# The first ten jobs of a fused RWKV kernel: token mixing moved from VectorE into the weights of keys and receptance

## The reference

```python
for l in range(L):
    h = layernorm(x, ln1_w[l], ln1_b[l])
    hh = time_shift(h)                       # the token before
    xk = h * tmk[l] + hh * (1 - tmk[l])
    xv = h * tmv[l] + hh * (1 - tmv[l])
    xr = h * tmr[l] + hh * (1 - tmr[l])
    k = jnp.einsum('btc,oc->bto', xk, Wk[l])
    v = jnp.einsum('btc,oc->bto', xv, Wv[l])
    sr = jax.nn.sigmoid(jnp.einsum('btc,oc->bto', xr, Wr[l]))
    rwkv = sr * wkv(time_decay[l], time_first[l], k, v)
    x = x + jnp.einsum('bto,co->btc', rwkv, Wo[l])
    ...
```

## Time and profile before

| | |
|---|---|
| median of three runs | 1414.1 us (1412.24 to 1419.84) |
| the profiled execution | 1414.5 us, its span 1413.1 us |
| PE busy | 1305.1 us (92%) |
| DVE busy | 1280.8 us (91%) |
| ACT busy | 1253.0 us (89%) |
| POOL busy | 1179.1 us (83%) |
| granted clock of PE, mean | 0.982 of full speed |
| chain of work that ended last | PE 63%, DVE 24%, ACT 3%, POOL 2% |

### The profile page before, as it was taken

One profiled execution on the slowest core, in us unless ns is written; L12 is line 12 of the kernel. 1 busy time (PEld: TensorE's weight loads), 2 busy tenths in 40 slices (PEclk: granted clock), 3 DMA queues, 4 the chain that ended last, 5 costly groups with the idle time before them and its releaser, 6 DMA issues.

```text
span 1413.1 us, 23624 instructions
## 1 busy us (share of the span) xinstructions
PE 1305.1 (92%) x7245; PEld 931.7 (66%) x7245; DVE 1280.8 (91%) x2185; ACT 1253.0 (89%) x2525; POOL 1179.1 (83%) x1227
## 2 busy tenths in 40 slices
PE   2568899999999999999999999989999999889996
PEld 1235567767666766666666776767677888666775
DVE  6999999999999999999999999569999666699995
ACT  6789999999999999999999998977777888967864
POOL 6999999999999999999998999879988534478874
PEclk9879999999999999999999999999999999999999
DMA  7000000001000000000000000010000000001001
GB/s 230 0 1 1 1 2 1 1 2 32 1 2 1 1 1 1 1 1 1 1 1 1 1 1 16 24 31 22 17 1 1 1 1 1 1 8 31 23 29 33
DMA packets 26924, 18.55 MB, mean 13 GB/s; under 512 B 1072, under 2 KB 26160, under 8 KB 26800
## 3 DMA queue, kind: packets, MB, share of 16 engines
q1 hardware_dynamic: 26800, 17.05, 4.1%
HBM read 12.85 MB, written 4.19 MB: 12 GB/s over the span
## 4 chain that ended last, share of the span: by engine, by line
PE 63%; DVE 24%; issue 7%; ACT 3%; POOL 2%; DMA 0%; DVEq 0%; SPq 0%; ACTq 0%; POOLq 0%
PE ps L1129 14%; PE ps L1112 13%; PE ps L1029 4%; PE ps L1119 4%; PE ps L1099 3%; PE ps L1082 3%; PE ps L1068 3%; PE ps L1075 3%; PE ps L1076 3%; DVE hsc L248 3%; PE ps L1238 2%; PE ps L1167 2%; PE ps L1220 2%; DVE W L455 2%; DVE W L485 2%
## 5 line engine op out<-in xcount | busy, mean ns | idle before, releaser
L1112 PE MATMUL ps<-xk,W 128*128 128x512 f32 x512 | 266.3, 603 | 1.4 <-DVE W L455 1.4
L1129 PEld LDWEIGHTS ps<-W,kf 128*128 128x128 f32 x2048 | 244.9, 192 | 31.2 <-issue 30.1
L1129 PE MATMUL ps<-W,kf 128*128 128x128 f32 x2048 | 250.4, 276 | 0.0
L748 ACT ACTIVATE z<-X,ln_rs 128x128 f32<-128x128 f32 x512 | 233.0, 667 | 4.3 <-POOL ln_rs L597 4.3
L855 ACT ACTIVATE kf<-ps 128x512 f32<-128x512 f32 x256 | 195.9, 765 | 3.1 <-PE ps L1112 3.1
L1029 PE MATMUL ps<-idn,z 128*128 128x128 f32 x664 | 106.1, 285 | 61.4 <-DVE aa L358 39.5
L1029 PEld LDWEIGHTS ps<-idn,z 128*128 128x128 f32 x664 | 83.3, 147 | 119.2 <-issue 61.2
L862 ACT ACTIVATE kf<-kf 128x1024 f32<-128x1024 f32 x128 | 158.1, 1235 | 0.0
L1112 PEld LDWEIGHTS ps<-xk,W 128*128 128x128 f32 x512 | 88.0, 194 | 58.6 <-issue 56.6
L704 POOL TENSOR_TENSOR W<-W,hsc 128x704 f32<-128x704 f32 x64 | 88.7, 1386 | 45.1 <-DVE W L485 45.1
L595 POOL TENSOR_TENSOR ln_rs<-ln_rs,mhalf 128x8 f32<-128x8 f32 (+1 forms) x70 | 124.5, 1779 | 0.0
(11 more groups left out here) (168 smaller groups left out, 3986.9 us busy)
## 6 DMA issues: line engine op xcount, KB each, us to landing
X<-x_in SPq DMA_DIRECT2D x16, 256.0 KB, 6.9
xi<-x_in SPq DMA_DIRECT2D x16, 256.0 KB, 2.9
out<-X SPq DMA_DIRECT2D x16, 256.0 KB, 2.3
W<-weights SPq DMA_DIRECT2D x4, 832.0 KB, 8.4
W<-fp4w SPq DMA_DIRECT2D x1, 560.0 KB, 3.7
row<-rows SPq DMA_DIRECT2D x1, 192.0 KB, 3.0
wqkv<-qkv SPq DMA_DIRECT2D x1, 96.0 KB, 5.9
idn<-ident SPq DMA_DIRECT2D x1, 64.0 KB, 2.8
```

Source lines behind the costliest of these rows:

```text
L748: last = e.activation(chunk(dst, j), chunk(src, j), ACT.Identity, bias=rs[:, 1, j:j + 1], scale=rs[:, 0, j:j + 1])
L1112: e.matmul((pF0, pF1)[f % 2][:, :], w_of(r, WCK + f), xk[r % 2][:, :], start=True, stop=True).then_inc(kf_mm[f], 1)
L1129: last = e.matmul(chunk(pKV, j), kf[r % 3][:, f, j * 128:(j + 1) * 128], w_of(r, WCV + f), start=f == 0 and j == 0, stop=f == 3, skip_grou ...
```

## The change

For jobs 0 to 9 (all of layer 0) keys and receptance are computed as the values are: each as two products on the unmixed h1, one with the weights times tm on h1[:, 1:], the other with the weights times (1 - tm) on h1[:, :-1]. These four matrices WE lie in `big` and are written by four multiplications of 128x128 in `prepare_layer` for layer 0; omt now holds 1 - tm for all three factors. In jobs 0 to 9 `mix_t`, `mix_rt` and `sub_dh1` do nothing. h1 gets a third buffer, and the waits of `keep_h1` reach back one job further. `tanh_r` gets a wait, since the tile sr is no longer written by `mix_rt` before. A wait in `keep_hq` goes; GAP has the value of NB.

```diff
+EARLY = 10
+GAP = NB
...
-        h1, h2 = ring("h1", 2, [128, T + 1]), ring("h2", 2, [128, T + 1])
+        h1, h2 = ring("h1", 3, [128, T + 1]), ring("h2", 2, [128, T + 1])
...
+        WE = big[:, 0, :].rearrange("p (k c) -> p k c", k=4)
...
-        PADS = 3 + 10
+        PADS = 3 + 11
...
-                e.tensor_scalar(omt[:, :], vec[:, TMV, :], -1.0, 1.0, ALU.mult, ALU.add).then_inc(omt_done, 1)
+                e.tensor_scalar(omt[:, :, :], vec[:, TMK:TMR + 1, :], -1.0, 1.0, ALU.mult, ALU.add).then_inc(omt_done, 1)
...
+                if l == 0:
+                    for k, (matrix, mix) in enumerate(((WK, TMK), (WR, TMR))):
+                        e.tensor_scalar(WE[:, 2 * k, :], wk(matrix), vec[:, mix, 0:1], None, ALU.mult)
+                        e.tensor_scalar(WE[:, 2 * k + 1, :], wk(matrix), omt[:, mix - TMK, 0:1], None, ALU.mult).then_inc(we_done, 1)
...
             def mix_t(r):
-                if 0 <= r < NR:
+                if EARLY <= r < NR:
...
             def mix_rt(r):
-                if 0 <= r < NR:
+                if EARLY <= r < NR:
...
             def sub_dh1(r):
-                if 0 <= r < NR:
+                if EARLY <= r < NR:
...
             def keep_h1(r):
                 if 0 <= r < NR:
                     w.wait_ge(consts, PADS)
-                    w.wait_ge(v_mm, r - 1)
-                    w.wait_ge(xt_done, r - 1)
-                    w.wait_ge(xr_done, r - 1)
+                    w.wait_ge(v_mm, r - 2)
+                    w.wait_ge(k_done, min(r - 2, EARLY))
+                    w.wait_ge(r_mm, min(r - 2, EARLY))
+                    w.wait_ge(xt_done, r - 2 - EARLY)
+                    w.wait_ge(xr_done, r - 2 - EARLY)
                     w.wait_ge(turned1, r + 1)
...
             def tanh_r(r):
                 if 0 <= r < NR:
+                    w.wait_ge(p_done, r - 2)
                     w.wait_ge(r_mm, r + 1)
...
-                    w.wait_ge(p_turned, NT * NB if n >= NB else 0)
...
             def keys(r):
...
-                    w.wait_ge(xt_done, r + 1)
-                    e.matmul(pK[:, :], w_of(r, WK), xt[r % 2][:, :], start=True, stop=True).then_inc(k_done, 1)
+                    if r < EARLY:
+                        w.wait_ge(we_done, 1)
+                        w.wait_ge(h1_done, r + 1)
+                        e.matmul(pK[:, :], WE[:, 0, :], h1[r % 3][:, 1:T + 1], start=True, stop=False)
+                        e.matmul(pK[:, :], WE[:, 1, :], h1[r % 3][:, 0:T], start=False, stop=True).then_inc(k_done, 1)
+                    else:
+                        w.wait_ge(xt_done, r + 1 - EARLY)
+                        e.matmul(pK[:, :], w_of(r, WK), xt[r % 2][:, :], start=True, stop=True).then_inc(k_done, 1)
...
             def receptance(r):
                 if 0 <= r < NR:
                     w.wait_ge(*bR.hand_over(sr_done, r + 1))
-                    w.wait_ge(xr_done, r + 1)
-                    e.matmul(pR[:, :], w_of(r, WR), sr[r % 3][:, :], start=True, stop=True).then_inc(r_mm, 1)
+                    if r < EARLY:
+                        w.wait_ge(we_done, 2)
+                        w.wait_ge(h1_done, r + 1)
+                        e.matmul(pR[:, :], WE[:, 2, :], h1[r % 3][:, 1:T + 1], start=True, stop=False)
+                        e.matmul(pR[:, :], WE[:, 3, :], h1[r % 3][:, 0:T], start=False, stop=True).then_inc(r_mm, 1)
+                    else:
+                        w.wait_ge(xr_done, r + 1 - EARLY)
+                        e.matmul(pR[:, :], w_of(r, WR), sr[r % 3][:, :], start=True, stop=True).then_inc(r_mm, 1)
```

More of the change, by code:

```diff
@@ L33 @@
 LN2_LAG = 6
-ATT_AT, FFN2_AT, TICKS = FFN_AT + NB, FFN_AT + 2 * NB, FFN_AT + 3 * NB + 18
+EARLY = 10
+GAP = NB
+ATT_AT, FFN2_AT, TICKS = FFN_AT + NB, FFN_AT + NB + GAP, FFN_AT + 2 * NB + GAP + 18
 class Waits:
@@ L105, in hybrid_program @@
         wneg = sb("wneg", [128, L])
-        omt = sb("omt", [128, L])
+        omt = sb("omt", [128, 3, L])
         row = sb("row", [128, 3, 128])
@@ L163, in hybrid_program @@
         xi_here = [sem("xi_here0"), sem("xi_here1")]
-        consts, ew_done, wneg_done, omt_done, w_mixed = [sem(k) for k in ("consts", "ew", "wneg", "omt", "w_mixed")]
+        consts, ew_done, wneg_done, omt_done, w_mixed, we_done = [sem(k) for k in (
+            "consts", "ew", "wneg", "omt", "w_mixed", "we")]
         in_w, in_x = sem("in_w"), sem("in_x")
@@ L211, in att_job @@
         def att_job(t):
-            return t - ATT_AT if ATT_AT <= t < FFN2_AT else None
+            return t - ATT_AT if ATT_AT <= t < ATT_AT + NB else None
         def vector():
@@ L239, in prepare_layer @@
                 w.wait_ge(omt_done, 1)
-                e.tensor_scalar(W2[:, l, :], wk(WV), omt[:, l:l + 1], None, ALU.mult).then_inc(w_mixed, 1)
+                e.tensor_scalar(W2[:, l, :], wk(WV), omt[:, TMV - TMK, l:l + 1], None, ALU.mult).then_inc(w_mixed, 1)
                 e.tensor_scalar(wk(WO), wk(WO), -0.5 * LEAD, None, ALU.mult).then_inc(w_mixed, 1)
@@ L629, in sub_dh1 @@
             def sub_dh1(r):
-                if 0 <= r < NR:
-                    w.wait_ge(xt_done, r - 1)
-                    w.wait_ge(xr_done, r - 1)
+                if EARLY <= r < NR:
+                    w.wait_ge(xt_done, r - 1 - EARLY)
+                    w.wait_ge(xr_done, r - 1 - EARLY)
                     w.wait_ge(h1_done, r + 1)
-                    e.tensor_tensor(dh1[r % 2][:, :], h1[r % 2][:, 1:T + 1], h1[r % 2][:, 0:T], ALU.subtract).then_inc(dh1_done, 1)
+                    e.tensor_tensor(dh1[r % 2][:, :], h1[r % 3][:, 1:T + 1], h1[r % 3][:, 0:T], ALU.subtract).then_inc(dh1_done, 1)
             def add_den(r):
@@ L787, in keep_h1 @@
                     w.wait_ge(consts, PADS)
-                    w.wait_ge(v_mm, r - 1)
-                    w.wait_ge(xt_done, r - 1)
-                    w.wait_ge(xr_done, r - 1)
+                    w.wait_ge(v_mm, r - 2)
[3 more added lines that the diff above has]
+                    w.wait_ge(xr_done, r - 2 - EARLY)
                     w.wait_ge(turned1, r + 1)
-                    e.activation(h1[r % 2][:, 1:T + 1], pT[:, :], ACT.Identity, bias=v_of(r, LN1B),
+                    e.activation(h1[r % 3][:, 1:T + 1], pT[:, :], ACT.Identity, bias=v_of(r, LN1B),
                                  scale=v_of(r, LN1W)).then_inc(h1_done, 1)
@@ L874, in f_z @@
                     w.wait_ge(v_mm, NR)
-                    w.wait_ge(xt_done, NR)
-                    w.wait_ge(xr_done, NR)
+                    w.wait_ge(xt_done, NR - EARLY)
+                    w.wait_ge(xr_done, NR - EARLY)
                     w.wait_ge(f_turned, n - 2)
@@ L1074, in values @@
                     w.wait_ge(h1_done, r + 1)
-                    e.matmul(pV[:, :], w_of(r, WV), h1[r % 2][:, 1:T + 1], start=True, stop=False)
-                    e.matmul(pV[:, :], w2_of(r), h1[r % 2][:, 0:T], start=False, stop=True).then_inc(v_mm, 1)
+                    e.matmul(pV[:, :], w_of(r, WV), h1[r % 3][:, 1:T + 1], start=True, stop=False)
+                    e.matmul(pV[:, :], w2_of(r), h1[r % 3][:, 0:T], start=False, stop=True).then_inc(v_mm, 1)
             def receptance(r):
```

8 lines of the change are left out of this document (4 added, 4 removed).

## The result

| | before | changed |
|---|---|---|
| median of six runs | 1417.0 us (1412.2 to 1419.8) | 1407.1 us (1403.0 to 1410.7) |
| profiled execution, its span | 1414.5, 1413.1 us | 1406.6, 1405.2 us |
| mean granted clock | 0.982 | 0.988 |

The ratio is 0.9938, with a 95% interval of 0.9919 to 0.9956: faster, by a little more than the half per cent that a measurement can tell. The medians differ by 9.9 us, and the interval stands for 6 to 11.5 us; execution against execution the gain is 7.9 us where the sum of the prediction said 11.5. The time, 1407.1 us, lies above the 1401 to 1405 that were forecast.

The account below looks back on a forecast made before the run. DVE alone was to bound the kernel to about 104 us, PE and ACT after 190 us, ACT nearly without slack between. 9.5 + 2.3 - 0.3 = 11.5 us; 1414.5 - 11.5 = 1403.0 us, range 1401 to 1405.

Parts of the forecast that it names:

- Rival D: Early intervals: slower, PE at half clock becomes the limit; 16.8 us more, less 4.3 gained, 1427 us; chance 0.04.
- Rival A: Behind job 6: ACT does not cap, DVE sets the pace through job 9; 13.5 us gained, 1401.0 us; chance 0.13.
- Rival B: Early jobs: POOL caps, its 1.0 us per job decides instead of 1.32; 7.8 us gained, 1406.7 us; chance 0.16.
- rival C: Head absorbs it: job 0 gains nothing, ACT holds DVE from interval 3 on; 4.1 us gained, 1410.4 us; chance 0.10.
- the start: Jobs 0 and 1: first scan 0.8 us earlier, held by PE's transposes at 20.07; 1.7 us for both jobs.
- what the two mixings of a job give back: Jobs 2 to 6, DVE alone limiting: 0.66 us per mixing, 1.32 per job, 6.6 us in all.
- the preparations: Layers 1 and 2, intervals 1 and 5: DVE's multiplications shorten once POOL's subtraction is gone; 1.2 us for both.
- the 2.3 us behind job 6: From 104.4 to 190 us ACT caps; only its waits, 2.1 and 0.2 us, can be had.
- the added multiplications: Head, layer 0's preparation: four of 128x128 on DVE, 0.9 us, covered by DVE's 1.62 us wait for ACT.
- the pair: Layers 1 and 2: L241 on DVE meets POOL's subtraction; apart, about 0.8 us comes back in each.
- PE's part: Interval 8: PE's work with two added products grows to 14.82 us against ACT's 14.5; 0.3 us taken off.
- The list of what would show it: Intervals 2 to 4 1.3 us shorter, DVE gapless to 100 us, clock over 0.85, ACT idle under 0.5 us to 190.

Follow-up runs that it names:

- mixing_kept: Changed kernel with DVE's mixings and POOL's subtraction of jobs 0 to 9 still computed but unused; ratio 0.9987 to the kernel before.
- one_product: Changed kernel with the second product of keys and receptance left out in jobs 0 to 9; ratio 0.9951 to the kernel before.
- subtraction_kept: Changed kernel with POOL's subtraction still computed for jobs 0 to 9, its result unused; ratio 0.9941 to the kernel before.
- early8: Changed kernel with the added products for jobs 0 to 7 only, jobs 8 and 9 mixed on DVE again; ratio 0.9934 to the kernel before.
- before_prep_late: Kernel before, without the change, with the preparations of layers 1 to 3 moved to steps 20, 24 and 28; ratio 0.9958 to the kernel before.
- stats_between: Changed kernel with init_stats moved on DVE from ahead of gate to between rwkv and arg_r; ratio 0.9935 to the kernel before.
- keys_first: Changed kernel with keys(t-5) moved ahead of ff_values(t-13, 0) in PE's order, all work kept; ratio 0.9945 to the kernel before.
- prep3_late: Changed kernel with layer 3's preparation moved eight steps later, into the steady jobs; ratio 0.9939 to the kernel before.

## Why the prediction was right and wrong

**Right:** the frame. DVE sets the pace to about 95 us, and what is saved there arrives at the end in full: the 8.2 us at scan 9 are there at scan 63, with 13.1 us per job in between. PE's products cost nothing by themselves, nor do the third buffer and the added waits, which mixing_kept holds too. Rival D fell: the granted clock from 25 to 100 us rose from 0.82 to 0.91. The rows of that stretch, before, changed, one_product and mixing_kept:

```profile
25.00:100.00 75.00, 44.03 (x121) 21.87 (x120) 74.49 (x123) 60.31 (x124) 68.42 (x81) 0.82 0.05 15
```

```profile
25.00:100.00 75.00, 55.01 (x160) 26.93 (x160) 73.40 (x124) 63.28 (x130) 61.88 (x78) 0.91 0.05 13
```

```profile
25.00:100.00 75.00, 48.82 (x133) 25.26 (x134) 73.72 (x124) 63.23 (x130) 63.00 (x78) 0.80 0.05 16
```

```profile
25.00:100.00 75.00, 53.53 (x144) 26.09 (x144) 74.47 (x123) 60.31 (x124) 68.76 (x83) 0.82 0.06 16
```

Shorter intervals alone left it at 0.80, and the added products alone at 0.82; both together gave 0.91, and 0.89 to 0.95 in the other profiles that have both.

Rival A fell too: behind job 6 came 1.3 us and not its 4.0. Rival B fell with subtraction_kept, though its 1406.7 is close to what was measured: the right number for the wrong reason. Of rival C the first half fits the number (scan 0 came no earlier), though not for its reason, as the start shows below, and the second didn't hold.

**Wrong:** the size, 11.5 us where 7.9 came. Four terms of the sum were too large: what the two mixings of a job give back, the preparations, the 2.3 us behind job 6, and the start. By the scans they make 3.3 us:

| term | forecast | measured |
|---|---|---|
| jobs 0 and 1 (to scan 1) | 1.7 | 0.3 (1.0 in early8's profile; 1.3 against before_prep_late's) |
| five intervals of two mixings | 6.6 | 6.0 |
| preparations of layers 1 and 2 | 1.2 | 0.65 |
| behind job 6 | 2.3 - 0.3 | 1.3 |
| sum | 11.5 | 8.2 |

*The start.* DVE's idle time covered the added multiplications, as forecast. PE and DVE of the changed kernel, at keys(0) and the first scan:

```profile
21.22 1.08 PE L1039 MATMUL ps<-idn,z 128*128 128x128 f32 x4 [3.28 <-ACT z L756]
22.09 1.92 PE L1080 MATMUL ps<-h,big 128*128 128x512 f32 x2
23.80 1.91 PE L1081 MATMUL ps<-h,big 128*128 128x512 f32 x2
```

```profile
15.08 0.28 DVE L251 TENSOR_SCALAR big<-W,vec 128x128 f32<-128x128 f32 x1
...
18.90 0.69 DVE L294 TENSOR_TENSOR xi<-xi,row 128x512 f32<-128x512 f32 x1 [1.62 <-ACT xi L756]
...
25.85 1.22 DVE L323 TENSOR_TENSOR_SCAN pp<-wneg,ps 128x512 f32<-128x512 f32 x1 [0.97 <-PE ps L1081]
```

The transposes that 20.07 stood for in the earlier trace rows came at 21.22, and keys(0) followed them as forecast, with two products 1.71 us apart. The order was right and its anchor, these transposes, was late by 1.15 us. About 0.4 of it came with the inputs (POOL's first operation waits until 12.42, before until 12.01), and 0.1 is POOL's L600 and L601 for in_rs (0.30 and 0.49 us, before 0.24 and 0.29), which now run beside the added multiplications. The other 0.6 is one instruction on POOL. Its timeline, changed, then before, then before_prep_late:

```profile
12.89 1.65 POOL L603 TENSOR_TENSOR ln_rs<-ln_rs,mhalf 128x4 f32<-128x4 f32 x1
```

```profile
12.48 1.04 POOL L595 TENSOR_TENSOR ln_rs<-ln_rs,mhalf 128x4 f32<-128x4 f32 x1
```

```profile
12.96 1.66 POOL L595 TENSOR_TENSOR ln_rs<-ln_rs,mhalf 128x4 f32<-128x4 f32 x1
```

The first power, of 4 elements a row, takes 1.04 us in the kernel before and 1.65 or 1.66 in all twelve others, before_prep_late among them, which has nothing of the change at its start. In these twelve DVE's multiplication of the normalisation (L294, in the kernel before L286) starts 0.02 us behind it, and in the kernel before 0.05 us behind. Whether that is the cause wasn't tested, but the change isn't: the profile that the forecast was worked out from had an early start. before_prep_late has its anchor at 21.06 and its first scan at 26.30. From anchor to scan it takes 5.24 us, the kernel before 5.23, and the changed kernel 4.63 (3.95 to 4.23 in the profiles whose second product is shorter than 1.9 us). So the order itself gained 0.6 us or more, near the 0.8 of the forecast; of the 1.4 us that this term misses, 1.0 is the start of that one profile. Interval 0 gave 0.87 of the 0.9 that stood for job 1. Without the second product, at half clock, the scan came 1.1 us earlier still (one_product, 24.75).

*The mixings.* 1.2 us an interval, not 1.32. The price by start to start was right for the instructions that went, but the one taken out from between L387 and L337 had covered a wait of 0.12 us (0.59 to 0.71) for a semaphore of the instruction just ahead, which the sum had put at nothing and stats_between could only shift.

*The preparations.* Right in kind and too large, 1.2 us where 0.65 came. In layer 1 the pair was misread: the subtraction met the multiplication of 128x512, L242 (1.27 us, after the change L246 with 0.41), and L241 met another POOL operation, so its successor L245 still takes 1.30 us at 43.08. In layer 2 the forecast pair did come apart (1.06 to 0.21 us). But in both the preparation now began beside the POOL operation ahead, and its first multiplication grew, from 0.43 to 0.71 and from 0.26 to 0.87 us. The Trainium skill (SBUF — State Buffer, section "Who interferes with whom") has such meetings as waits for a shared port; these rows agree, and show that their cost hangs on the place.

*Behind job 6.* This step failed as reasoning: the prediction took ACT's waits, 2.3 us (2.5 with 0.2 for L323's result, which it left out), as what could be had, as if a faster DVE could remove each. DVE's and ACT's waits of the changed kernel, 104.4 to 190 us:

```profile
DVE pp L323 <- PE ps L1081: 2.1, 2, 1.4
```

```profile
ACT h L859 <- PE ps L1039: 0.9, 1, 0.9
ACT er L834 <- DVE er L337: 0.2, 1, 0.2
```

One wait of ACT, 0.9 us, stayed. It stands behind scan `aa` of the interval that holds layer 3's preparation. DVE's work between the square it gets from ACT and that scan is longer than ACT's work in the same stretch; neither engine starting earlier shortens it, as one_product and keys_first show, where DVE waits for ACT ahead of that stretch and ACT for DVE behind it. Taking DVE's work out of that stretch does: in prep3_late this wait is gone, and ACT gained 1.5 us. PE's part was right in kind (14.82 us, as computed) but it costs nothing of the sum, since the chain over ACT and DVE would have taken the same time.

The list of what would show it: DVE without a gap to 100 us (but for 0.3 us in job 0, for ACT's L834), the clock over 0.85, DVE then waiting for keys, all as listed. ACT's idle time was to be under 0.5 us and is 1.1; intervals shorter by 1.3 were shorter by 1.2. One row was read loosely: the granted clock is under 9 tenths in slices 2 and 3 alone, not in 2 to 5.

## What to carry to other kernels

Cut the start of a pipelined kernel at one instruction per job and compare two kernels by those starts: they repeat within hundredths where medians wander by several microseconds, and they show whether a gain made early is still there at the end. Where another engine sets the pace, check the gain on an instruction of that engine: in prep3_late the scans gained 2.8 us and ACT 1.5. Before counting a wait of an engine as recoverable, follow it back to its own releaser: where that one in turn waits for the first engine, the loop through both sets the time, and only work inside the loop counts. And when one engine bounds only the fill of the pipeline, look there for work with no due time: moving three small preparations to the steady part brought about half as much as the whole change (from scan 0 to 16, 4.2 us on top of 8.8).

## What the hardware showed that was not expected

- Two instructions behind one another on DVE, of which the second waits for the first one's semaphore, start 0.71 to 0.73 us apart; with another instruction between, the same form is followed after 0.59 to 0.60.
- A multiplication on DVE of 128x512 by a scalar takes 0.41 us alone and 1.27 (up to 1.50) beside POOL operations; of 128x128 0.22 and 1.30. That is how a preparation of 0.9 us (layer 0) becomes one of 1.5 to 3.4.
- Some hundredths of a microsecond between the starts go with long instructions on both sides: POOL's power of 128x4 took 1.65 us where DVE's L294 started 0.02 us behind it and 1.04 where it was 0.05, and DVE's L387 took 1.60 us started with POOL's L672 and 0.68 started 1.2 us behind it. No run varied the offset alone.
- The granted clock of the start rose from 0.82 to 0.91 only where PE had the added products and the intervals were shorter, both; with either alone it was 0.80 and 0.82.
